# Two-layer conditioned attention on one core: second-layer query and key projections in the last slots of the step ahead, and middle parts written by VectorE from PSUM

## The reference

```
layer 0:  a = x + attention(rmsnorm(x, cond))          # 16 heads of 16, softmax over all 256 keys
          x = x + a + swiglu(rmsnorm(a, cond))         # hidden size 1024
layer 1:  q, k, v = x Wq, x Wk, x Wv                   # no norm ahead of the projections
          scores masked by mask_SxS_bk1                # True hides a key
          x = x + (rmsnorm(attention @ Wo) * scale * (1 + s) + shift)
```

## Time and profile before

| | us |
|---|---|
| median of 3 runs | 1015.0 (1012.26 to 1016.26) |
| the profiled execution's own time | 1008.46 |
| its span in the profile | 1006.6 |
| TensorE busy | 909.2 (90%) |
| VectorE busy | 570.3 (57%) |
| ScalarE busy | 547.5 (54%) |
| GpSimd busy | 415.2 (41%) |
| mean granted TensorE clock | 0.967 of full |

### The profile page before, as it was taken

How to read it: one execution, slowest core, us unless ns; L and a number is a source line. 1 busy time by engine, 2 the same in 40 slices (tenths; PEclk the granted TensorE clock), 3 DMA queues, 4 the chain that set the end, 5 groups by cost and what they waited for, 6 DMA issues and landing times.

```text
span 1006.6 us, 24326 instructions
## 1 busy us (share of the span) xinstructions
PE 909.2 (90%) x8188; PEld 780.6 (78%) x8188; DVE 570.3 (57%) x1104; ACT 547.5 (54%) x1130; POOL 415.2 (41%) x633
## 2 busy tenths in 40 slices
PE   3578899999999999999999999999999789888874
PEld 3456698898888988988889889889887677777653
DVE  3366556557555565575565756545455455555541
ACT  2246556546455565464554665554556566666652
POOL 5223344443443444434334344344444454444522
PEclk9779999999999999999999999999999999999997
DMA  6555423322332233223322242232437576576611
GB/s 204 110 106 122 91 64 75 75 65 59 66 86 42 63 73 73 63 58 68 84 42 63 69 91 65 65 76 66 94 74 167 119 160 147 142 166 144 157 36 34
DMA packets 83070, 91.29 MB, mean 91 GB/s; under 512 B 7776, under 2 KB 70016, under 8 KB 83008
## 3 DMA queue, kind: packets, MB, share of 16 engines
q1 hardware_dynamic: 83008, 90.50, 39.8%
HBM read 60.30 MB, written 29.36 MB: 89 GB/s over the span
## 4 chain that ended last, share of the span: by engine, by line
PE 73%; issue 8%; DVE 7%; ACT 5%; POOL 3%; DMA 1%; SPq 1%; POOLq 0%; DVEq 0%; ACTq 0%
PE work L525 11%; PE work L527 11%; PE work L526 11%; PE pvps L622 8%; PE s2ps L606 7%; PE s1ps L583 5%; PE work L710 4%; PE acc L525 3%; PE acc L526 2%; PE acc L527 2%; PE work L656 2%; PE s1ps L568 2%; PE work L718 1%; DVE rest L919 1%; DVE th L959 1%
## 5 line engine op out<-in xcount | busy, mean ns | idle before, releaser
L1055 ACT ACTIVATE E<-s2ps 128x512 f32<-128x512 f32 x384 | 214.1, 596 | 184.2 <-PE s2ps L606 110.8
L882 DVE TENSOR_REDUCE nmax<-s1ps 128x2 f32<-128x512 f32 x256 | 163.9, 682 | 32.1 <-PE s1ps L583 31.9
L525 PE MATMUL work<-xch,Gh 128*128 128x256 f32 x512 | 154.5, 302 | 0.0
L959 DVE SCALAR_TENSOR_TENSOR th<-th,work 128x256 f32<-128x256 f32 x128 | 53.8, 420 | 168.7 <-ACT th L1073 168.7
L1328 POOL TENSOR_TENSOR hl<-hf,hh 128x256 fp32r<-128x256 f32 x128 | 94.9, 742 | 131.0 <-PE acc L527 77.3
L526 PE MATMUL work<-xcl,Gh 128*128 128x256 f32 x512 | 147.1, 287 | 0.0
L527 PE MATMUL work<-xch,Gl 128*128 128x256 f32 x512 | 146.9, 287 | 0.0
L606 PE MATMUL s2ps<-stack 100*128 100x256 bf16 x768 | 127.7, 275 | 2.1 <-DMA stack<-rows 2.0
L875 DVE TENSOR_REDUCE nmax<-s1ps 128x4 f32<-128x512 f32 x128 | 85.6, 685 | 36.5 <-PE s1ps L568 36.4
L525 PEld LDWEIGHTS work<-xch,Gh 128*128 128x128 f32 x512 | 99.3, 194 | 8.2 <-issue 6.6
L622 PE MATMUL pvps<-E,vaug 128*32 128x256 f32 x1536 | 97.5, 387 | 6.3 <-ACT E L1055 4.0
(11 more groups left out here) (131 smaller groups left out, 2149.1 us busy)
## 6 DMA issues: line engine op xcount, KB each, us to landing
stack<-scr SPq DMA_DIRECT2D x64, 384.0 KB, 4.6
stack<-scr SPq DMA_DIRECT2D x64, 256.0 KB, 5.2
scr<-qp SPq DMA_DIRECT2D x64, 192.0 KB, 2.3
scr<-kp SPq DMA_DIRECT2D x64, 192.0 KB, 2.3
stack<-scr SPq DMA_DIRECT2D x64, 128.0 KB, 5.6
X<-xT SPq DMA_DIRECT2D x16, 256.0 KB, 4.5
yT<-crm SPq DMA_DIRECT2D x16, 256.0 KB, 5.2
stack<-rows SPq DMA_DIRECT2D x196, 4.0 KB
```

The costliest lines, as they stand in the source:

```text
L525: mm(out, lh, rh, start=first, stop=False, skip_group_check=True)
L882: v.tensor_reduce(nmax[:, g // 4, qh, 2 * (g % 4):2 * (g % 4) + 2], s1ps[u % 2][:, :].rearrange("p (h t) -> p h t", h=2), AX_X, ALU.max, n ...
L959: v.scalar_tensor_tensor(th[:, i % 2, :], th[:, i % 2, :], 1.0, bank[:, 0:T], ALU.add, ALU.mult).then_inc(silu_ready, 1)
L1055: a.activation(E[:, exp_slot(st.L["B2"], st.full, g, kh), :], s2ps[g % 2 if short else u % 2][:, :], ACT.Exp, scale=SCORE_SCALE).then_inc( ...
```

## The change

For layer 1, Q and K of n = s+3 (not s+2) are projected in step s, in slots 6 and 7, for s = 13 to 28. On TensorE they stand in front of that slot's `swiglu_up`; on VectorE, ScalarE and GpSimd their parts stand at the end of the slot (the key's low part behind the shift split at the step's end). The layer-0 projections stay in slots 1 and 2. For both layers VectorE computes bank minus high part twice: once with a bf16 result, which is the middle part, and once more into `rest`; ScalarE's middle cast goes. GpSimd's low part waits for both. The swaps of Wq and Wk move from slots 4 and 6 of step 13 to slots 3 and 5.

```diff
+    found["A0"] = 0 if layer(s + 2) == 0 else None
+    found["A1"] = 1 if layer(s + 3) == 1 else None
...
+def projected(L, g):
+    if g in (1, 2) and L["A0"] is not None:
+        return "QK"[g - 1], 2
+    if g in (6, 7) and L["A1"] is not None:
+        return ("Q1", "K1")[g - 6], 3
+    return None
...
     uses = []
     for g in range(SLOTS):
-        if g == 0 and L["A"] == 1:
-            uses.append("Q")
...
+        if g >= 6 and projected(L, g):
+            uses.append(projected(L, g)[0])
         if L["C2"] is not None:
             uses.append(f"F{g}")
...
-        SWAPS = {(13, 4): 0, (13, 6): 1, (14, 4): 2, (16, 4): 3}
+        SWAPS = {(13, 3): 0, (13, 5): 1, (14, 4): 2, (16, 4): 3}
...
-            def qk_projection(st, use, w):
-                after(pe, n_lo, st.n(2) + 1)
+            def qk_projection(st, use, ahead):
+                w = "QK".index(use[0])
+                if st.s0 + ahead == B:
+                    pe.wait_ge(swap_lo, w + 1)
+                after(pe, n_lo, st.n(ahead) + 1)
                 bank, full = open_bank(st, use)
...
-                    if g == 0 and L["A"] == 1:
-                        query_projection(st)
...
-                    if g == q_slot(L, 1):
-                        qk_projection(st, "K", 1)
+                    if projected(L, g):
+                        qk_projection(st, *projected(L, g))
...
-            def qk_split(st, use, parts, hi_at, high):
+            def qk_split(st, use, ahead):
...
+                hi = parts[:, hi_at, :, :].rearrange("p c t -> p (c t)")
+                v.tensor_tensor(parts[:, 1, :, :].rearrange("p c t -> p (c t)"), bank[:, :], hi, ALU.subtract)\
+                 .then_inc(mid, 1)
+
+                after(dve, k_low if use[0] == "Q" else q_low, n if use[0] == "Q" else n + 1)
+                v.tensor_tensor(flat(rest[:, :, :]), bank[:, :], hi, ALU.subtract).then_inc(free, 1)
...
                     if L["C2"] is not None:
                         swiglu(st, g)
+                    if g >= 6 and projected(L, g):
+                        qk_split(st, *projected(L, g))
...
-            def middle(st, use, parts, mid):
-                b, k = st.bank(use)
-                after(act, work_free[b], k + 1)
-                a.copy(parts[:, 1, :, :], rest[:, :, :]).then_inc(mid, 1)
+            def qk_high(st, use, ahead):
...
-                    if g == q_slot(L):
-                        middle(st, "Q", qp, q_mid)
-                    if g == q_slot(L, 1):
-                        middle(st, "K", kp, k_mid)
+                    if g >= 6 and projected(L, g):
+                        qk_high(st, *projected(L, g))
...
+            def qk_low(st, use, ahead):
...
                 after(pool, mid, n + 1)
+                b, k = st.bank(use)
+                after(pool, work_free[b], k + 1)
...
+                    if g == 6 and projected(L, g):
+                        qk_low(st, *projected(L, g))
                 if L["B1"] is not None:
                     shift_split(st, 1)
+                if projected(L, 7):
+                    qk_low(st, *projected(L, 7))
```

More of the change, by code:

```diff
@@ L114, in bank_uses @@
             uses.append("sh1")
-        if g == 1 and L["A"] == 0:
+        if g == 1 and projected(L, g):
             uses.append("Q")
@@ L120, in bank_uses @@
             uses.append("Wo")
-        if g == q_slot(L, 1):
+        if g == 2 and projected(L, g):
             uses.append("K")
@@ L485, in step @@
                     load_raw(3)
+                load_swap(3)
                 load_swap(4)
@@ L910, in o_split @@
                  .then_inc(free, 1)
-            def qk_split(st, use, parts, hi_at, high):
-                n = st.n(2)
+            def qk_split(st, use, ahead):
+                n = st.n(ahead)
+                parts, hi_at, high, mid = (qp, 0, q_high, q_mid) if use[0] == "Q" else (kp, 2, k_high, k_mid)
                 bank, free = opened(st, use)
                 after(dve, high, n + 1)
-                after(dve, k_low if use == "Q" else q_low, n if use == "Q" else n + 1)
-                v.tensor_tensor(flat(rest[:, :, :]), bank[:, :],
-                                parts[:, hi_at, :, :].rearrange("p c t -> p (c t)"), ALU.subtract).then_inc(free, 1)
+                hi = parts[:, hi_at, :, :].rearrange("p c t -> p (c t)")
[3 more added lines that the diff above has]
+                v.tensor_tensor(flat(rest[:, :, :]), bank[:, :], hi, ALU.subtract).then_inc(free, 1)
             def attention_residual(st):
@@ L1092, in shift_store @@
                 a.copy(nT, bank[0:24, 0:P].bitcast(BF16)).then_inc(free, 1)
[L1094 to L1097, removed]
-            def middle(st, use, parts, mid):
-                b, k = st.bank(use)
-                after(act, work_free[b], k + 1)
-                a.copy(parts[:, 1, :, :], rest[:, :, :]).then_inc(mid, 1)
+            def qk_high(st, use, ahead):
+                bank, _ = opened(st, use)
+                parts, hi_at, high, written = (qp, 0, q_high, q_written) if use[0] == "Q" else (kp, 2, k_high, k_written)
+                after(act, written, 32 * st.n(ahead))
+                a.copy(parts[:, hi_at, :, :].rearrange("p c t -> p (c t)"), bank[:, :]).then_inc(high, 1)
             def step(st):
@@ L1140, in step @@
                             shift_store(st, 0)
[L1141 to L1146, removed]
+                    if g <= 2 and projected(L, g):
+                        qk_high(st, *projected(L, g))
                     if g == 2 and L["R"] is not None:
@@ L1228, in stack_constants @@
                 p.memset(kst[i][PARTS:MASKED, :, :].bitcast(F32), 0.0).then_inc(stack_ones, 1)
-            def low_q(st, parts, hi_at, lo_at, mid, low):
-                n = st.n(2)
+            def qk_low(st, use, ahead):
+                n = st.n(ahead)
+                parts, lo_at, mid, low = (qp, 2, q_mid, q_low) if use[0] == "Q" else (kp, 0, k_mid, k_low)
                 after(pool, mid, n + 1)
+                b, k = st.bank(use)
+                after(pool, work_free[b], k + 1)
                 p.tensor_tensor(parts[:, lo_at, :, :], rest[:, :, :], parts[:, 1, :, :],
```

35 lines of the change are left out of this document (12 added, 23 removed).

## The result

The changed kernel takes **1035.9 us** (median of 4 runs, 1035.3 to 1037.3), the kernel before in the same series 1013.6 (4 runs, 1009.2 to 1016.3). The ratio is 1.021, with a 95% interval from 1.017 to 1.026: slower, clear of the noise; whether it is more than 2% slower the interval leaves open. The forecast was 1024, its range ended at 1031. The profiled execution took 1035.99 us, its span is 1033.9; before, they were 1008.46 and 1006.6, so 27.3 us of span are to be found.

A forecast was written before the change was run, and what follows sets the result against it. TensorE was taken as the bound: up to about 740 us only its idle time can be won. Terms 3 + 11.3 - 3.6 - 1.5 = +9 us on the median gave 1024 us, range 1014 to 1031.

The forecast's parts named there:

- a sign of being wrong: Prediction counts as wrong if bcC starts without a wait, or the layer-1 period falls below 16.7 or stays above 17.4.
- Layer 0, +3 us: Twelve layer-0 steps: VectorE's second subtraction frees Q's bank 0.61 later, so T2 newly waits 0.25 us; bounds 0 to 8.
- Steps 13 to 17, +11.3 us: Slot 6 and after: bcC waits 2.19 us in four steps for Q1's bank, then step 17 waits 1.8 and 0.7.
- Layer 1, -3.6 us: Steps 18 to 29: twelve intervals between output projections each win 0.30 us of 17.43; bounds -10.4 to +2.
- T2 starts at 4.6 and Wo at 6.65: Layer-1 step, us after pair 1's values: T1b waits 0.6 for the key's `rest`, VectorE's division follows, then T2 and Wo.
- The twelfth interval of the forecast: Output projection of step 17 to that of 18, counted among the twelve layer-1 intervals winning 0.30 us each.
- DMA, -1.5 us: Slot 0: first-half rows get 1.5 us of a second projection more, so the 1.48 us wait for them goes.
- layer 1 loses: Rival, chance 0.14: T1b's wait delays the second half's row DMAs, half a microsecond lost in 12 steps; 1034, or 1029.
- without the stall at bcC: Rival, chance 0.10: Q1's parts are ready when F6 is done; the sum falls by 8.8 to 1015, no change.
- with a full layer 1: Rival, chance 0.07: projections fill all 2.0 us of TensorE idle time per layer-1 step, 24 us won; 1004 us.
- VectorE's burst doesn't bind: Rival, chance 0.17: in layer 1 each of 12 intervals wins 0.87 us; sum +2.4, 1017, no measurable change.
- rival spacing: Two VectorE subtractions start the full 0.69 us apart, not 0.61; the sum would be some 5 us more.

## Why the prediction was wrong, point by point

**The sign was right, the size was not:** +9 forecast, +22 measured in the medians (1035.9 against 1013.6) and +27.5 in the profiled executions. The period rose above 17.4, to 18.47, which the text itself had named as a sign of being wrong.

**Layer 0, +3 us: right.** Waits of 0.17 to 0.42 where 0.25 was said, and a step that is 0.20 and 0.37 us longer in turn, 0.28 on average; times 12 that is 3.4. (The text read a margin of 1.18 to 1.24 in eleven steps; the last of them has 1.30.) Up to step 13 only 1.3 us of it show, since some steps of this part take 41.1 to 41.7 us and not 39.6 to 40.0, in every kernel, and the changed one has three of them where the kernel before has five. That VectorE's second subtraction is the cause is shown by the runs without it in layer 0, whose steps are back at 39.59.

**Steps 13 to 17, +11.3 us: right in its mechanism, a little too high.** The forecast was 2.19 four times, 1.8 and 0.7; the trace shows 1.94 four times, 1.57 and 0.39, 9.7 in all. Each is 0.2 to 0.3 us under its forecast. The last step of the count was "the bank is open for TensorE 0.84 later"; bcC starts 0.74 after the subtraction. The rest is a difference of measure: the text counted from start to start, and the profile's idle time begins only at the end of the matmuls before. The run with the parts ahead of the feed-forward work shows that it was the order on the two engines.

**Layer 1, -3.6 us: here the prediction failed.** The step of the text was "T2 starts at 4.6 and Wo at 6.65". Counted from the values, the trace has T1b at 3.06 (2.85 forecast), T2 at 5.99 and Wo at 8.07. From T2 to Wo it is 2.08, as the text said. What is missing are 1.2 us between T1b and T2: 2.93 where the forecast had 1.75. I let only VectorE's chain set T2, and left out that TensorE's own queue has bcR ahead of it. bcR stands in the spare bank behind sh1; ScalarE frees that bank by the rows' copy; the copy stands behind the exponentials, which wait for scores that TensorE issues after sh1. The 1.52 us of the key, which the text books as won, were the cover of just this. bcR waits 0.98 to 1.05 us in each of 11 steps (19 to 29); taking the copy ahead took 0.77 off each period and gave 10.5 us back in the median. The rest of the 1.04 is mostly T1b's wait, which the forecast did have: with it at 0.21 the period is 17.40 to 17.48. VectorE's chain was right to 0.1 to 0.4 us in each place (K1's first subtraction at 1.73 for 1.4, its last product for T2 done at 4.84) but did not set the end. In place of -3.6 stands 11 times 1.04, +11.4. The twelfth interval of the forecast (17 to 18) is 1.17 longer, but it holds K1's 1.57, which is counted above. A slip in the sum changes nothing: 8.47 - 1.52 - 6.1 is 0.85, not 0.87.

**DMA, -1.5 us: not there.** The text said that the wait for rows goes, since they get "the 1.5 us of a second projection more". A wait of 1.39 us stayed, and the 1.27 of step 19 came on top. The two runs that take the rows ahead of the store show that their place behind it sets most of this wait; the forecast had not looked at what stands ahead of them there.

**Sum by what was measured:** 3.4 + 9.7 + 11.4 + 0 = 24.5 of the 27.3 us between the two spans. The parts cut it otherwise: 1.3 up to step 13, then 9.4, 11.9 and, in the last steps, which the forecast left out, 4.7. Most of the latter is TensorE's busy time at a lower granted clock (+3.2 us at 0.76 against 0.85), and two DMAs are late by 0.6 and 1.1 us. Among all kernels the last three intervals between output projections go from 12.6 to 21.6 us. This was not forecast, and why the clock is lower there stays **open**. The profiled execution of before, 1008.46, is also faster than each of the four runs beside the result (1009.2 to 1016.3), so part of the 27.3 may be the spread of single executions; the first three parts alone come to 22.6, near the 22 of the medians.

**The rivals.** That layer 1 loses (chance 0.14, 1029 to 1034) had the right side, and its time was near, but by another way: it was T1b's wait that should push the rows' DMAs. The wait of T1b is real (0.55) and cost little: with it at 0.21 the total moved by less than can be measured. The rivals without the stall at bcC and with a full layer 1 are refuted by the trace after. The rival that VectorE's burst doesn't bind was half right: the burst costs 0.2 to 0.3 us of period (17.70 against 17.40 to 17.48), but another wait bound.

## What to carry to other kernels

Work that is moved away was also the cover for what stands behind it in the same queue: walk through every later instruction of that queue, not only those of the chain that you mean to shorten, and for each ask which engine frees its bank and what stands ahead of that on the freeing engine. When work is moved into a slot, put its short, bank-freeing parts on the other engines ahead of the slot's long chain. And when a compute wait becomes shorter, look at once for the DMA that is due next, and at what stands ahead of it on its queue.

## What the runs showed of the hardware

Two subtractions of VectorE from PSUM (128x512), each 0.68 to 0.69 us long by the profile, start 0.60 apart when nothing stands between them (864.93 to 865.53, 867.74 to 868.34). The Trainium skill (VectorE: DVE Perf Modes, Terms) says that the next instruction can't issue until the pipe of the one before is empty. The prediction worked out the full 0.69 from it as the rival spacing; these starts, as the row of before, don't bear that reading out.

DMAs of 4 KB that stand behind a 256 KB store on the same queue were up to 1.7 us late for their use. Put ahead of it and issued at the same time (791.64 in place of 791.63), they cost 0.36 us in all of layer 1, and the whole kernel gained 4.4 us (1010.7 to 1006.3) in one version and 10.6 (1012.3 to 1001.7) in another.

A wait that cuts a group of matmuls in two costs more than the idle time that the profile puts beside it: T1a and T1b in two pieces are busy for 0.65 + 0.66 us, in one piece for 1.10, so 0.21 us more. In a layer-1 step idle times account for 0.69 of the 1.05 us lost; only the distance between starts shows all of it.

In layer 0, where TensorE is busy for 98.87 of 100 us, single steps take 41.1 in place of 39.6 us at a lower granted clock (before: 0.96 from 251.51 to 292.63, 1.00 from 211.91 to 251.51), in the kernel before as in the changed ones. Which steps these are differs from kernel to kernel, so two traces can differ by a few microseconds up to the same place for that alone.
